# Halves of the tokens taking turns ahead of two wide attentions, in a one-core chain of eight sublayers

## Chip, cores and metric

The kernel runs on one core of a Trainium2 chip, in one launch. The metric is the device time of the launch in microseconds, as the median over runs.

## The reference, cut to what matters

1024 tokens (4 batches of 256) of width 128 pass through four gated pairs of cross attention and feed-forward. Every sublayer has the form `x = x + tanh(g) * f(...)`; the attentions and the first feed-forward work on a normalised x.

```python
x = x + tanh(g_xattn[1]) * L1_xattn(layernorm(x), ctx, mask, ...)   # 16 heads of 64: relu(scores)^2, normalised
x = x + tanh(g_ffn[1])   * L1_ffn(layernorm(x), ...)
x = x + tanh(g_xattn[2]) * L2_xattn(layernorm(x), ctx, ctx)         # 16 heads of 8, no weights
x = x + tanh(g_ffn[2])   * L2_ffn(layernorm(x), kernel, bias, a, b) # x @ (int4(kernel) + a @ b) + bias
x = x + tanh(g_xattn[3]) * L3_xattn(layernorm(x), ctx, ...)         # 16 heads of 64: clipped softmax
...
def L3_xattn(latents, context):
    lat, cx = layernorm(latents, ln_l_w, ln_l_b), layernorm(context, ln_c_w, ln_c_b)
    q, k, v = lat @ Wq, split(cx @ Wkv)
    attn = softmax(clip(q @ k.T * 64 ** -0.5, -11, 11))
    return (attn @ v) @ Wo + bo
```

L3_xattn normalises what it is given, so x is normalised twice there; the kernel does it in one norm with a changed epsilon.

## The kernel before

Each engine has its own program, in order, and semaphores tie them. The residual `res` lies tokens-first in eight tiles of 128 tokens; tiles 0 to 3 are the first half, 4 to 7 the second. Channels-first copies (`xf`, `xh`, `xl`) are 128x1024, a half is 512 columns. A product that must be precise takes three matmuls of split operands, high and low part (`mm3`, L185 to L189); `bank(k)` is one of eight PSUM banks of 512 columns.

A norm goes through five engines' queues. VectorE takes the statistics (`norm_sums`, L235), GpSimd the power (`norm_pool`, L271), VectorE a Newton step and the tiles (`norm_tiles`, L245), TensorE four transposes per half (`norm_pe`, L283), ScalarE a copy of the bank (`norm_act`, L302), and VectorE the low part (`norm_dve_split`, L315). `stream` (L278) is products of the identity with itself, whose result nobody reads. In these functions both halves go through a step before the next step begins.

A wide attention (call c = 0 for L1, c = 1 for L3) has 16 heads in eight pairs of heads by four batches: 32 groups g, two to a turn x, four turns to a weight block i. `project(x)` makes queries and keys of head pair x // 2 for half x % 2, in banks 6 and 7. ScalarE copies them as high parts (`high`, L1029), VectorE subtracts the low parts (`low`, L1142). `scores(g)` (L884) needs the queries and keys of batch g % 4, so groups 0 and 1 need the first half alone. VectorE bounds the scores (`bound`, L1151), ScalarE makes the weights (`weights`, L1050), TensorE the value products (L907), GpSimd adds the weights for the denominators (L1091). Ahead of the loop TensorE does

```python
            for h in range(2):
                pe.wait_ge(s_xs, 2 * splits(m) + h + 1)
                project(h)
            at("va", 2)
            scores(0)
            at("va", 4)
            scores(1)
            project(2)
```

VectorE does `low(0)`, `low(1)`, `bound(0)`, `bound(1)`, and ScalarE `high(0)`, `high(1)`, `weights(0)`, `weights(1)`. The attention adds its output into `xn`, which VectorE sets to zero (c = 0, L2101) or to the bias bo (c = 1, L2153) ahead of the loop.

Between the narrow attention L2 and the wide L3, TensorE transposes the normalised context (`context_pe`, L808), ScalarE applies weight and bias (L819, L820) and VectorE subtracts the low part (L824). The quantised feed-forward L2_ffn is eight products of 128 columns, each two records in the trace (L336); VectorE adds the bias (L2142), then the gated residual (L1246), then takes the statistics. These are norms 5 and 6, and the projections of the context's values (`wide_first_values_pe`, L863) stand behind both.

## Time and profile before

| | |
|---|---|
| median of 3 runs | 853.56 us (850.42 to 855.19) |
| the profiled execution | 858.75 us, its span 856.9 us |
| busy: TensorE, VectorE, ScalarE, GpSimd | 780.0, 626.2, 451.7, 197.0 us |
| first stretch (ahead of wide attention c = 0) | about 168 to 190 us |
| second stretch (ahead of wide attention c = 1) | about 519 to 551 us |
| GpSimd's additions L1091 | 64, mean 1358 ns |

The span is from the first to the last instruction of the profiled execution, and its own time includes what lies around that. Matmuls are pipelined and their ends modelled, so the busy time of TensorE (PE) is no peak rate. PEld is its weight load, DVE is VectorE, ACT ScalarE, POOL GpSimd. A bracket at a row's end names the idle time before the instruction and what ended it.

### The profile page before, as it was taken

How to read it: one execution, taken by the hardware profiler on the slowest of the kernel's cores; microseconds unless marked ns; L12 is line 12 of the kernel's file. 1: busy time of each engine (PE TensorE's matmuls, PEld its weight loads, DVE VectorE, ACT ScalarE, POOL GpSimd, SP SyncE). 2: the span in 40 equal slices, each digit the busy share in tenths (PEclk: the TensorE clock that was granted, in tenths of full speed). 3: DMA queues.
4: the chain of work that ended last, by engine and by line, in shares of the span. 5: the costliest groups of instructions: out<-in, count | busy, mean ns of one | idle time of the engine just before them, and what ended most of it. 6: DMA issues, size and time to landing. Idle time of an engine off the chain costs nothing. (4 is left out here: it accounts for less than half of the span.)

```text
span 856.9 us, 14220 instructions
## 1 busy us (share of the span) xinstructions
PE 780.0 (91%) x5206; PEld 556.2 (65%) x5206; DVE 626.2 (73%) x1168; ACT 451.7 (53%) x681; POOL 197.0 (23%) x163
## 2 busy tenths in 40 slices
PE   5998889989999899999989887899998879999996
PEld 4654556666677587777766545666775757777774
DVE  6678576667766587888776877776657868778876
ACT  3466352246655316999825665565554145555553
POOL 3000020023545321222220001146445201111112
PEclk9999789989999897999999999999999989999998
DMA  9100000130220200000270000002201000000000
GB/s 347 71 2 1 2 0 1 48 149 2 52 51 2 50 1 1 0 1 0 99 313 1 2 1 2 2 1 52 50 20 32 2 1 0 1 1 0 0 1 24
DMA packets 3660, 29.64 MB, mean 35 GB/s; under 512 B 560, under 2 KB 912, under 8 KB 2064
## 3 DMA queue, kind: packets, MB, share of 16 engines
q1 hardware_dynamic: 3600, 28.83, 10.0%
q8 instruction: 40, 0.66, 0.3%
q14 instruction: 20, 0.16, 0.1%
HBM read 28.20 MB, written 0.62 MB: 34 GB/s over the span
## 5 line engine op out<-in xcount | busy, mean ns | idle before, releaser
L187 PE MATMUL banks<-normed_t_high,work_split 128*128 128x512 f32 x250 | 110.1, 440 | 12.3 <-DVE work L1942 3.9
L1091 POOL TENSOR_TENSOR work<-work 128x512 f32<-128x512 f32 x64 | 86.2, 1358 | 134.0 <-ACT work L1053 134.0
L189 PE MATMUL banks<-normed_t_high,work_split 128*128 128x512 f32 x250 | 101.1, 404 | 0.0
L188 PE MATMUL banks<-normed_t_low,work_split 128*128 128x512 f32 x250 | 100.9, 404 | 0.0
L712 DVE TENSOR_REDUCE work<-banks 128x2 f32<-128x512 f32 x128 | 84.7, 688 | 18.3 <-PE banks L454 15.4
L1829 ACT ACTIVATE work<-banks 128x512 f32<-128x512 f32 x68 | 40.6, 598 | 70.2 <-PE banks L189 70.2
L276 POOL TENSOR_TENSOR ln_rstd<-ln_var_eps,minus_half_and_newton 128x4 f32<-128x4 f32 x16 | 17.2, 1076 | 248.3 <-DVE ln_var_eps L242 239.6
L1942 DVE TENSOR_TENSOR work<-work,banks 128x512 f32<-128x512 f32 x68 | 46.6, 687 | 36.0 <-ACT work L1829 35.6
L187 PEld LDWEIGHTS banks<-normed_t_high,work_split 128*128 128x128 f32 x250 | 48.0, 192 | 34.2 <-issue 17.6
L187 PE MATMUL banks<-work_split 128*128 128x512 f32 x148 | 64.2, 434 | 6.3 <-DVE work_split L1905 4.9
L907 PE MATMUL banks<-work 128*64 128x256 f32 x512 | 64.1, 388 | 2.2 <-ACT work L1053 1.7
L1688 DVE TENSOR_TENSOR work_split<-work,work_split 128x512 fp32r<-128x512 f32 x64 | 53.2, 832 | 16.0 <-ACT work_split L1614 15.3
L189 PE MATMUL banks<-work_split 128*128 128x512 f32 x148 | 58.5, 395 | 0.0
L188 PE MATMUL banks<-work_split 128*128 128x512 f32 x148 | 58.5, 395 | 0.0
L454 PE MATMUL banks<-work_split 32*128 32x256 f32 x256 | 54.1, 330 | 4.6 <-DVE work L712 3.0
L895 PEld LDWEIGHTS banks<-work_split 64*128 64x128 f32 x768 | 49.8, 194 | 12.7 <-issue 7.3
L1860 POOL TENSOR_TENSOR sublayer_out_t<-sublayer_out_t,work 128x512 f32<-128x512 f32 x18 | 23.6, 1312 | 148.6 <-DVE work L1916 146.7
L895 PE MATMUL banks<-work_split 64*128 64x256 f32 x768 | 56.5, 295 | 0.0
L188 PEld LDWEIGHTS banks<-normed_t_low,work_split 128*128 128x128 f32 x250 | 48.3, 193 | 12.1 <-issue 3.4
L189 PEld LDWEIGHTS banks<-normed_t_high,work_split 128*128 128x128 f32 x250 | 48.2, 193 | 11.7
L1053 ACT ACTIVATE work<-work,small_operands 128x1024 f32<-128x1024 f32 x32 | 36.8, 1150 | 34.7 <-DVE work L1157 34.1
L1145 DVE TENSOR_TENSOR work_split<-banks,work_split 128x512 fp32r<-128x512 f32 x32 | 21.8, 683 | 45.3 <-ACT work_split L1033 45.3
(288 smaller groups left out, 1752.6 us busy)
## 6 DMA issues: line engine op xcount, KB each, us to landing
raw_b<-in_wf SPq DMA_DIRECT2D x1, 6528.0 KB, 19.1
raw_a<-in_wf SPq DMA_DIRECT2D x1, 4096.0 KB, 13.1
raw_b<-reciprocal_rows SPq DMA_DIRECT2D x6, 512.0 KB, 6.0
raw_a<-reciprocal_rows SPq DMA_DIRECT2D x6, 512.0 KB, 6.4
raw_a<-in_wf SPq DMA_DIRECT2D x1, 2048.0 KB, 15.5
raw_b<-in_wb SPq DMA_DIRECT2D x1, 2048.0 KB, 19.7
raw_a<-in_wb SPq DMA_DIRECT2D x1, 2048.0 KB, 7.8
small_operands<-in_small SPq DMA_DIRECT2D x1, 1530.0 KB, 11.5
```

Source lines behind the costliest of these rows:

```text
L187: nc.tensor.matmul(o, w[0], m[0], start=start, stop=False)
L188: nc.tensor.matmul(o, w[0], m[1], start=False, stop=False)
L189: return nc.tensor.matmul(o, w[1], m[0], start=False, stop=stop)
L454: last = nc.tensor.matmul(ps[:, 7 - n % 2, e * S:(e + 1) * S], a_y[a_rows(j), t * P:(t + 1) * P], half(a_ky, x % 4)[a_rows(j), pair * S:(p ...
L712: nc.vector.tensor_reduce(a_nm[:, t:t + 2, j], bank(7 - n % 2).rearrange("p (e k) -> p e k", e=2), AX.X, ALU.max, negate=True).then_inc(A[ ...
L895: last = nc.tensor.matmul(ps[:, 2 * (g % 2) + h, kb * S:(kb + 1) * S], w_k[kt][rows, keys], w_q[qt][rows, b * S:(b + 1) * S], start=n == 0 ...
L907: last = nc.tensor.matmul(ps[DH * h:DH * (h + 1), 4, (b % 2) * S:(b % 2 + 1) * S], w_v[:, 2 * b + kb, (2 * p + h) * DH:(2 * p + h + 1) * D ...
L1053: nc.scalar.activation(p, p, func, bias=bias, scale=0.125).then_inc(W["p"].sem, 1)
L1091: nc.gpsimd.tensor_tensor(w_ps[g % 2].rearrange("p (h q) -> p h q", h=2), v[:, :, 0, :], v[:, :, 1, :], ALU.add).then_inc(W["ps"].sem, 1)
L1688: nc.vector.tensor_tensor(g_a[n % 4][1], g_af[n % 4], g_a[n % 4][0].bitcast(F32), ALU.subtract)\
L1829: nc.scalar.activation(k_sg[n % 2], bank(n % 2), ACT.Silu).then_inc(K["sg"].sem, 1)
L1942: nc.vector.tensor_tensor(k_af[n % 2], k_sg[n % 2], bank(2 + n % 2), ALU.mult).then_inc(K["a"].sem, 1)
```

## The change

In both stretches a half goes through all its steps before the other. Ahead of either wide attention TensorE transposes and projects the first half, then transposes the second, makes the scores of groups 0 and 1, and then projects the second half; the third projection follows the first value products inside the loop. VectorE's `low(1)` stands behind the first two bounds, and the clearing of `xn` behind the second weight block's split in the loop's first turn. ScalarE copies the first value tiles before the norm's halves. Between L2 and L3 the context's low part goes to GpSimd under its own semaphores; the bias of the quantised layer becomes a matmul of the identity with the broadcast bias, opening each bank's accumulation, and VectorE reads the sum straight into the residual (`back_half`). The order of norms 5 and 6 interleaves by half.

```diff
-        def context_low(dve, m, h):
-            dve.wait_ge(s_xf, 2 * m + h + 1)
-            nc.vector.tensor_tensor(half(cl, h), half(out_t, h), half(ch, h).bitcast(F32), ALU.subtract).then_inc(s_xs, 1)
+        def context_low(pool, h):
+            pool.wait_ge(s_cf, h + 1)
+            nc.gpsimd.tensor_tensor(half(cl, h), half(out_t, h), half(ch, h).bitcast(F32), ALU.subtract).then_inc(s_cl, 1)
...
                 for k in range(4):
                     x = 4 * i + k
                     pair(x)
+                    if x == 0:
+                        project(2)
                     next_scores(x)
...
-            for h in range(2):
-                pe.wait_ge(s_xs, 2 * splits(m) + h + 1)
-                project(h)
+
+            pe.wait_ge(s_ve, 2 * n + 1)
+            stream(6, 6)
+            norm_half_pe(pe, n, 0)
+            pe.wait_ge(s_xs, 2 * splits(m) + 1)
+            project(0)
+            stream(4, 5)
+            norm_half_pe(pe, n, 1)
             at("va", 2)
             scores(0)
             at("va", 4)
             scores(1)
-            project(2)
+            pe.wait_ge(s_xs, 2 * splits(m) + 2)
+            project(1)
...
-            for n in range(4):
-                value_tiles(n, n)
+            norm(0)
+            if c == 0:
+                norm(1)
             high(0)
+            if c == 1:
+                norm(1)
             high(1)
             weights(0)
             weights(1)
...
                     if x == 0:
                         wide_weights(dve, c, 1, raw, r0)
+                        clear()
...
             low(0)
-            low(1)
+            second()
             bound(0)
             bound(1)
+            low(1)
...
+        def quant_half_pe(pe, h):
+
+            pe.wait_ge(s_qw, 1)
+            pe.wait_ge(s_xf, 2 * 5 + h + 1)
+            nc.tensor.matmul(bank(6 + h).rearrange("p (t d) -> p t d", t=4), ident,
+                             col("quant_bias").unsqueeze(1).to_broadcast((P, 4, D)), start=True, stop=False)
+            for t in range(4):
+                last = nc.tensor.matmul(ps[:, 6 + h, t * P:(t + 1) * P], xf[:, (4 * h + t) * P:(4 * h + t + 1) * P],
+                                        q_w[:, :], start=False, stop=t == 3)
+            last.then_inc(s_rt, 1)
...
-            norm_pool(pool, 5)
-            norm_pool(pool, 6)
+            norm_half_pool(pool, 5, 0)
+            context_low(pool, 0)
+            norm_half_pool(pool, 5, 1)
+            norm_half_pool(pool, 6, 0)
+            context_low(pool, 1)
+            norm_half_pool(pool, 6, 1)
...
-            context_act(act, 5)
-            norm_act(act, 6, k=4, done=2 * splits(5))
-            norm_act(act, 7, w=col("ln_l_w"), b=col("ln_l_b"), k=4)
-            wide_act(act, 1, ACT.Exp, 0.0)
+            norm_half_act(act, 5, 0)
+            context_act(act)
+            wide_first_tiles_act(act, 1, 0)
+            norm_half_act(act, 5, 1)
+            wide_first_tiles_act(act, 1, 1)
...
-            order.step(nc.vector.memset(xn[:, :, :], 0.0))
...
+            dve.wait_ge(A["att"].sem, A["att"].at(1, NG, 0))
+            tokens_in(dve, order, 4, a_att, (1,))
+            norm_sums(dve, order, 5, 1, res)
+            back_half(dve, order, 3, 5, 0)
+            norm_sums(dve, order, 6, 0, res)
+            norm_tiles(dve, order, 5, 1, res, xn)
+            norm_tiles(dve, order, 6, 0, res, xn)
+            back_half(dve, order, 3, 5, 1)
+            norm_sums(dve, order, 6, 1, res)
+            norm_half_split(dve, order, 6, 0, xh, xl, False)
+            norm_tiles(dve, order, 6, 1, res, xn)
...
-            norm_pe(pe, 5, 6, k=4)
-            pe.wait_ge(s_qw, 1)
-            tokens_pe(pe, xf, q_w[:, :], ((s_xf, 2 * 6 + 1), (s_xf, 2 * 6 + 2)))
-            pe.wait_ge(s_xs, 2 * splits(5) + 2)
-            wide_first_values_pe(pe, 1)
-            norm_pe(pe, 6, 7, k=4)
-            wide_pe(pe, 1, 7, raw_a, RB3)
+            quant_half_pe(pe, 0)
+            wide_first_values_pe(pe, 1, 0)
+            stream(6, 7)
+            norm_half_pe(pe, 5, 1)
+            quant_half_pe(pe, 1)
+            wide_first_values_pe(pe, 1, 1)
+            wide_pe(pe, 1, 6, 6, raw_a, RB3)
```

The order on TensorE before, at the start of the first wide attention, from the last matmul of the second projection on (L189 of mm3 ends a projection, L895 are scores, L907 value products, L926 denominators):

```order
L189 MATMUL banks<-context_t_high,work_split 128x512
L895 MATMUL banks<-work_split 128x256 x24
L187 MATMUL banks<-normed_t_high,work_split 128x512
L188 MATMUL banks<-normed_t_low,work_split 128x512
L189 MATMUL banks<-normed_t_high,work_split 128x512
L187 MATMUL banks<-context_t_high,work_split 128x512
L188 MATMUL banks<-context_t_low,work_split 128x512
L189 MATMUL banks<-context_t_high,work_split 128x512
L907 MATMUL banks<-work 64x256 x8
L895 MATMUL banks<-work_split 128x256 x24
```

The same place in the change, from the first projection's last matmul on (L284 is `stream`, L300 the transposes, L910 scores, L922 value products):

```order
L189 MATMUL banks<-context_t_high,work_split 128x512
L284 MATMUL banks<-small_operands 128x128 x4
L300 MATMUL banks<-small_operands,normed_tokens 128x128 x4
L910 MATMUL banks<-work_split 128x256 x24
L187 MATMUL banks<-normed_t_high,work_split 128x512
L188 MATMUL banks<-normed_t_low,work_split 128x512
L189 MATMUL banks<-normed_t_high,work_split 128x512
L187 MATMUL banks<-context_t_high,work_split 128x512
L188 MATMUL banks<-context_t_low,work_split 128x512
L189 MATMUL banks<-context_t_high,work_split 128x512
L922 MATMUL banks<-work 64x256 x8
L187 MATMUL banks<-normed_t_high,work_split 128x512
```

Each projection moved one place back: the second from ahead of the scores to behind them, the third (it begins in the last row) from ahead of the first value products to behind them.

VectorE in the loop's first turn of the first wide attention, before (L1145 and L1148 are low parts, L1157 bounds, L1130 and L1135 the weights' split):

```order
L1157 SCALAR_TENSOR_TENSOR work<-banks,score_floor,raw_b 128x1024 x2
L1130 CAST work_split<-raw_b 128x768
L1135 TENSOR_TENSOR work_split<-raw_b,work_split 128x768
L1145 TENSOR_TENSOR work_split<-banks,work_split 128x512
L1148 TENSOR_TENSOR work_split<-banks,work_split 128x512
```

And in the change:

```order
L1182 SCALAR_TENSOR_TENSOR work<-banks,score_floor,raw_b 128x1024 x2
L1155 CAST work_split<-raw_b 128x768
L1160 TENSOR_TENSOR work_split<-raw_b,work_split 128x768
L2155 MEMSET normed_tokens 128x1024
L1170 TENSOR_TENSOR work_split<-banks,work_split 128x512
L1173 TENSOR_TENSOR work_split<-banks,work_split 128x512
```

The memset came from ahead of the first low parts; in the second wide attention a copy of the bias bo takes the same place.

## Rows read from the trace of the kernel before

**Rows 1.** Page, part 1: busy time, share of the span, instructions.
```profile
PE 780.0 (91%) x5206; PEld 556.2 (65%) x5206; DVE 626.2 (73%) x1168; ACT 451.7 (53%) x681; POOL 197.0 (23%) x163
```

**Rows 2.** Waits of TensorE from 196 to 320 us: total, times, longest.
```profile
PE banks L934 <- DVE normed_t L1172: 3.2, 1, 3.2
PE banks L187 <- ACT work L1047: 0.8, 3, 0.3
```

**Rows 3.** Timeline of TensorE, first stretch: start us, us, engine, line, operation, operands, [idle before <-releaser].
```profile
177.84 1.10 PE L299 MATMUL banks<-small_operands,normed_tokens 128*128 128x128 f32 x4 [0.52 <-DVE normed_tokens L256]
...
179.21 0.50 PE L187 MATMUL banks<-normed_t_high,work_split 128*128 128x512 f32 x1 [0.27 <-DVE normed_t_low L322]
...
180.91 0.63 PE L189 MATMUL banks<-context_t_high,work_split 128*128 128x512 f32 x1
...
183.56 0.77 PE L187 MATMUL banks<-normed_t_high,work_split 128*128 128x512 f32 x1 [2.02 <-DVE work_split L1148]
...
185.83 0.63 PE L189 MATMUL banks<-context_t_high,work_split 128*128 128x512 f32 x1
...
186.38 1.86 PE L895 MATMUL banks<-work_split 64*128 64x256 f32 x24
...
190.24 2.28 PE L907 MATMUL banks<-work 128*64 128x256 f32 x16 [0.40 <-ACT work L1053]
```

**Rows 4.** Slices of 1 us: busy shares, PEclk (the granted clock), DMA.
```profile
179.00:180.00 1.00, 0.79 (x3) 0.67 (x4) 0.55 (x2) 1.00 (x3) 0.00 (x0) 0.97 0.09 33
...
186.00:187.00 1.00, 1.00 (x8) 0.62 (x8) 0.53 (x1) 0.51 (x1) 0.00 (x0) 0.62 0.00 0
```

**Rows 5.** Timelines of VectorE and ScalarE, first stretch, by start.
```profile
179.47 2.06 ACT L1047 ACTIVATE work<-banks 128x512 f32<-128x512 f32 x4
...
180.46 0.91 DVE L2101 MEMSET normed_tokens<- 128x1024 f32 x1 [0.16 <-issue]
...
187.73 2.47 DVE L1157 SCALAR_TENSOR_TENSOR work<-banks,score_floor,raw_b 128x1024 f32<-128x1024 f32 x2
...
189.04 2.34 ACT L1053 ACTIVATE work<-work,small_operands 128x1024 f32<-128x1024 f32 x2 [1.95 <-DVE work L1157]
```

**Rows 6.** Timeline of TensorE, second stretch.
```profile
523.23 4.18 PE L281 MATMUL banks<-small_operands 128*128 128x128 f32 x36
...
528.63 2.02 PE L336 MATMUL banks<-quant_weights,normed_t 128*128 128x128 f32 x16
...
533.45 0.39 PE L187 MATMUL banks<-work_split,context_t_high 128*128 128x256 f32 x1 [2.80 <-DVE context_t_low L824]
...
542.37 0.50 PE L187 MATMUL banks<-normed_t_high,work_split 128*128 128x512 f32 x1 [1.62 <-DVE normed_t_low L322]
...
543.63 0.40 PE L189 MATMUL banks<-context_t_high,work_split 128*128 128x512 f32 x1
...
551.03 2.21 PE L907 MATMUL banks<-work 128*64 128x256 f32 x16 [0.41 <-ACT work L1053]
```

**Rows 7.** Timeline of VectorE, second stretch.
```profile
522.24 0.26 DVE L734 RECIPROCAL work<-banks 128x16 f32<-128x16 f32 x1 [2.76 <-PE banks L504]
...
528.30 0.69 DVE L824 TENSOR_TENSOR context_t_low<-sublayer_out_t,context_t_high 128x512 fp32r<-128x512 f32 x1
...
529.79 0.69 DVE L2142 TENSOR_TENSOR normed_tokens<-banks,small_operands 128x512 f32<-128x512 f32 x1 [0.80 <-PE banks L336]
...
543.29 0.69 DVE L2153 COPY normed_tokens<-small_operands 128x1024 f32<-128x1024 f32 x1
```

**Rows 8.** Durations of VectorE's split and tile lines, ns min/median/max, first and last start.
```profile
L1135 DVE TENSOR_TENSOR work_split<-raw_b,work_split x4: 957/1474/1927, 167.4 to 244.4; 128x768 fp32r<-128x768 f32 x4
...
L256 DVE TENSOR_SCALAR normed_tokens<-residual,ln_mean_var,ln_rstd x64: 328/344/1065, 6.8 to 680.6; 128x128 f32<-128x128 f32 x64
```

**Rows 9.** Timeline of TensorE at 168 us; the page's group of GpSimd's addition.
```profile
167.93 1.88 PE L1425 MATMUL banks<-work_split,small_operands 128*128 128x512 f32 x4
...
L1091 POOL TENSOR_TENSOR work<-work 128x512 f32<-128x512 f32 x64 | 86.2, 1358 | 134.0 <-ACT work L1053 134.0
```

More of the change, by code:

```diff
@@ L296, in norm_pe @@
             for h in range(2):
-                for t in range(4 * h, 4 * h + 4):
-                    pe.wait_ge(s_xn, NT * n + t + 1)
-                    last = nc.tensor.transpose(ps[:, k + h, (t % 4) * P:(t % 4 + 1) * P], src[:, t, :], ident)
-                last.then_inc(s_xt, 1)
-        def norm_act(act, m, f32=True, high=None, w=None, b=None, k=6, done=None):
-            for h in range(2):
-                act.wait_ge(s_xt, 2 * m + h + 1)
-                act.wait_ge(s_xs, 2 * splits(m) if done is None else done)
-                if f32 and w is None:
-                    ins = nc.scalar.activation(half(xf, h), bank(k + h), ACT.Copy)
-                elif f32:
-                    ins = nc.scalar.activation(half(xf, h), bank(k + h), ACT.Identity, bias=b, scale=w)
-                if high is not None:
-                    ins = nc.scalar.activation(half(high, h), bank(k + h), ACT.Copy)
-                ins.then_inc(s_xf, 1)
+                norm_half_pe(pe, n, h, src, k)
@@ new lines, in norm_half_pe, with norm_act, norm_half_act @@
+        def norm_half_pe(pe, n, h, src=xn, k=4):
+            for t in range(4 * h, 4 * h + 4):
+                pe.wait_ge(s_xn, NT * n + t + 1)
+                last = nc.tensor.transpose(ps[:, k + h, (t % 4) * P:(t % 4 + 1) * P], src[:, t, :], ident)
+            last.then_inc(s_xt, 1)
+        def norm_act(act, m, f32=True, high=None, w=None, b=None, k=6):
+            for h in range(2):
+                norm_half_act(act, m, h, f32, high, w, b, k)
+        def norm_half_act(act, m, h, f32=True, high=None, w=None, b=None, k=4):
+            act.wait_ge(s_xt, 2 * m + h + 1)
+            act.wait_ge(s_xs, 2 * splits(m))
+            if f32 and w is None:
+                ins = nc.scalar.activation(half(xf, h), bank(k + h), ACT.Copy)
+            elif f32:
+                ins = nc.scalar.activation(half(xf, h), bank(k + h), ACT.Identity, bias=b, scale=w)
+            if high is not None:
+                ins = nc.scalar.activation(half(high, h), bank(k + h), ACT.Copy)
+            ins.then_inc(s_xf, 1)
@@ L325, in back_pe, with norm_half_split @@
+        def norm_half_split(dve, order, m, h, hi, lo, from_bank=True, k=4):
+            dve.wait_ge(s_xf, 2 * m + h + 1)
+            src = bank(k + h) if from_bank else half(xf, h)
+            if not from_bank:
+                order.step(nc.vector.tensor_copy(half(hi, h), src))
+            nc.vector.tensor_tensor(half(lo, h), src, half(hi, h).bitcast(F32), ALU.subtract).then_inc(s_xs, 1)
         def back_pe(pe, ready, k):
@@ L1135, in wide_weights_low, with wide_dve @@
             nc.vector.tensor_tensor(w_w[i % 2][1], qkv, w_w[i % 2][0].bitcast(F32), ALU.subtract).then_inc(W["w"].sem, 1)
-        def wide_dve(dve, order, c, raw, r0, between, spare):
+        def wide_dve(dve, order, c, raw, r0, second, clear, between, spare):
             def at(name, n):
@@ L2170, in _ @@
             f0_pe(pe, 1)
-            wide_first_values_pe(pe, 0)
-            norm_pe(pe, 2, 2, k=4)
-            wide_pe(pe, 0, 2, raw_b, RB1)
+            for h in range(2):
+                wide_first_values_pe(pe, 0, h)
+            wide_pe(pe, 0, 2, 2, raw_b, RB1)
             norm_pe(pe, 3, 3)
```

97 lines of the change are left out of this document (42 added, 55 removed).

## The prediction

> **What bounds the kernel now.** I read the page first: TensorE is busy 780.0 of 856.9 us [rows 1]. That mean hides two kinds of place, so the waits of TensorE came next. From 196 to 320 us, which is most of a wide attention, its only long wait is 3.2 us near the attention's end [rows 2]; inside the loop over head pairs it hardly waits. So whatever delays the first pair delays the end one for one, and a head start is kept if nothing is added to the loop. The two stretches that the change rewrites lie before those loops: about 170 to 190 us, and 519 to 551 us. I walked both in the timelines, engine by engine.
>
> First stretch. TensorE transposes the second half while VectorE makes the first half's low part, projects the first half at 179.21, waits 2.02 us, projects the second at 183.56, scores from 186.38 and reaches the first value products at 190.24 [rows 3]. ScalarE's weights start at 189.04, as soon as VectorE's bound of the first scores (187.73, two in 2.47) is through [rows 5]. The granted clock is 0.97 and then lower in the slices from 179 us on, 0.62 as it comes back in slice 186 [rows 4]: between them the engine runs at 1.2 GHz. So the second projection lasts from 183.56 to 186.46, where six such products at 2.4 GHz take from 542.37 to 544.03, 1.66 us [rows 3, 6]; the first, 179.21 to 181.54, took 2.33 us [rows 3]. Together 1.9 us of this stretch is clock.
>
> Second stretch. VectorE is the chain: context's low part at 528.30, the bias added at 529.79 after waiting 0.80 for the quantised product, then the two halves' statistics and tiles until 539.6 [rows 7]. TensorE fills in with 36 records of identity products in 4.18 us (18 products of 0.23), waits 2.80 before 533.45, projects at 542.37 and reaches the first values at 551.03 [rows 6].
>
> **The sum, first stretch (+4.0 us).** Nothing before 179.21 moves: the same low part releases the same projection. Behind it now stand four identity products (0.93) and the second half's four transposes (0.7 with their tail), so these end at 179.21 + 1.40 + 0.93 + 0.7 = 182.3 at 2.4 GHz. ScalarE copies the second half, then query and key, at about 0.5 apiece [rows 5]; VectorE's three subtractions at some 0.61 apiece (0.69 alone, [rows 7]) end at 184.8. Scores start there, 1.5 us earlier than now. But the second projection stands behind both scores (1.62) and ends at 188.1, and on ScalarE the copies of that projection stand in front of the first weights: these start at 188.6, though their scores were bounded by 187.0. First values: 189.8 against 190.24, a gain of only 0.45. Then the third projection comes between the first values and the next scores: before, it ran in TensorE's wait, now it adds its whole 1.40. VectorE's bound of the next scores stands behind the low parts of that projection, which wait for ScalarE's copies of it: +0.4. The clearing of the tokens (0.91) stood in a wait of VectorE [rows 5] and now stands in the loop's first turn, behind the next weights' split, with the next low parts and bounds queued behind it: +0.9. Sum at 2.4 GHz: -0.45 + 1.40 + 0.4 + 0.9 = +2.3. I take the low clock to come back: TensorE does less ahead of 179.9 us than now, as the second half's transposes (1.10 us, [rows 3]) have gone from there. That gives back 1.7 of the 1.9 us, which the -0.45 had counted as gained. **+4.0**; ends: +2.3 (full clock) and +4.6 (clock low as long as now, scores and copies in it too).
>
> **The sum, second stretch (-2.4 us).** The first half's tiles for the quantised layer go into VectorE's 2.76 us wait for the last transposes [rows 7]: free. Transposes and ScalarE's copy (behind the context tiles) end at 523.8. The bias now costs TensorE a product of its own per half: two 128x512 products in plain float32 show as four records in 1.88 us, so 0.94 each [rows 9]; I take 0.9, bounded below by 0, if it fits a wait, and above by twice that at half clock. With four products of 0.25 the first half is back at 525.7 (now 529.65). VectorE then needs 0.79 for the residual, 1.40 for the statistics and, with the second half's tiles at 1.75, is at 529.7. Two subtractions of 0.6 and two bias additions of 0.7 have left it, 2.6 us. GpSimd's low part has no row of its own: the nearest is its 128x512 addition, mean 1.358 [rows 9]; lower bound 0.69, VectorE's own price [rows 7], upper bound 1.36 + 0.96 if it meets a VectorE instruction. It ends at 526.4, and the second half's power behind it on GpSimd at 527.5, before VectorE asks for it at 527.9: covered by 0.4 us. Transpose, copy, bias and products of the second half end at 532.5; then the second values (1.4), six identity products (1.4, and these, not data, are late next) and the first half's transposes to 535.9, ScalarE 0.8, VectorE's cast and low part 1.15: the first projection at 537.9 against 542.37, 4.5 earlier. The tail of the first stretch follows: scores at 540.9, second projection 542.8 to 544.5, first values at 546.2 against 551.03, 4.85 earlier. Then the loop takes +1.40 and +0.4 as above, and the bias copy (0.69, [rows 7]) that moves into it +0.7. **-2.4**; upper end -1.2, if the second context subtraction on GpSimd holds the tiles.
>
> That end is from rows: one tile instruction takes 344 ns in the median and 1065 at most, the split 957 at least and 1927 at most, and the long ones lie beside instructions of GpSimd [rows 8]. I keep 1.25, one GpSimd instruction, as the bound and 0 as the value, since the second context subtraction can start as the tiles end. The Trainium skill, SBUF — State Buffer, SBUF: two separate sides, says that VectorE in a two-port mode or with two SBUF inputs and GpSimd exclude each other for a whole instruction. By that rule the sum would be 1.25 higher in the worst order of arrival; the doubled split agrees, what the order will be no row shows.
>
> **Together** +4.0 - 2.4 = +1.6 us. The profiled execution took 858.75 us, 5.2 above the median of 853.56; put on the median it gives **855.2**. The cases of the sum reach from -0.1 to +3.4. A measurement of this kernel can tell some 0.5%, 4.3 us, from no change, so this is no change, chance 0.50.
>
> **Rivals.**
> 1. The loop has room (0.15). The head starts stay and the moved projection and clearing are absorbed: -0.45 - 4.85 = -5.3, **848.2**. For it: TensorE's busy time has gaps of tenths. Against: no wait over 0.8 us until the attention's end [rows 2].
> 2. GpSimd blocks VectorE (0.13), which ends slower. Three places: the quantised layer's tiles (1.25) and, in each attention's first turn, the split and the clearing, which now stand in a row beside GpSimd's additions (1.26 each beyond the sum): +3.8 on +1.6, **859.0**. It decides if a GpSimd addition starts before each of these; for it, the split that doubles already [rows 8].
> 3. The clock falls in both stretches (0.15): before the first projection TensorE now waits 1.9 us in either. +0.6 in the first and +1.0 in the second: **856.8**, and with the hold of the tiles 858.
> 4. It does not do what it says (0.07): scores in the first stretch no earlier than 186.4, as the streams and the second half's transposes eat the lead; +1.5 more: 856.7.
>
> **Numbers.** Faster by over 0.5%: 0.13 of rival 1, 0.04 of the rest, 0.17. Slower: 0.10 of rival 2, 0.08 of rival 3, 0.04 of the rest, 0.22. Within: 0.61. The range 848.5 to 859.5 takes in rival 2 and the sum's ends, and stops just short of rival 1.
>
> **What would show it.** Right: in the first attention the first value products at 190 to 192 us, with ScalarE's two projection copies directly ahead of the first weights; a projection between the first values and the next scores; in the second attention the first projection near 538 us, the first values near 546 us and the second pair only some 3 us earlier than before. Wrong: if TensorE shows waits inside the loop's later turns, room was there; if the second pair in the first attention starts by 196.3 us, the inserted projection cost nothing; if VectorE's tiles or splits show 1 us and more beside GpSimd, rival 2 holds; if the granted clock is full from 179 to 187 us, take 1.7 off.

## The result, and the profile after

The changed kernel takes 860.78 us (median of 5 executions, 857.9 to 863.3) against 853.56 (850.42 to 855.67, now with 5 executions too): ratio 1.0085, interval 1.0056 to 1.0113. It is 7.2 us slower; the forecast was 855.2 and no change, and the range ended at 859.5.

| | before | after |
|---|---|---|
| median | 853.56 us | 860.78 us |
| the profiled execution, its span | 858.75, 856.9 us | 857.9, 856.0 us |
| busy TensorE, VectorE, ScalarE, GpSimd | 780.0, 626.2, 451.7, 197.0 us | 775.0, 626.9, 452.9, 199.2 us |
| mean granted clock of the profiled execution | 0.958 | 0.969 |

The two profiled executions are level, though the medians are 7.2 us apart: the one of before took 5.2 us more than the median of its kernel, at a low mean clock, and the one after was the fastest of its five. So the spans say nothing here, and I compare stretches between landmarks. A runs from the second instruction `ln_var_eps` of norm 2 on VectorE (175.12 us before, 168.99 after) to the first value products of the turns 0, 1, 2 and 4 of the wide attention c = 0; B from the last reciprocal of the narrow attention (522.24, 520.66) to the same of c = 1. The expectations call turn 2 the third pair and turn 4 the fifth pair, and A the stretch from the power, or from the second statistics, of norm 2.

| us from the landmark | A: turn 0 | 1 | 2 | 4 | B: turn 0 | 1 | 2 | 4 |
|---|---|---|---|---|---|---|---|---|
| before | 15.12 | 21.12 | 26.87 | 42.32 | 28.79 | 34.73 | 40.39 | 55.34 |
| after | 15.99 | 23.51 | 30.70 | 46.14 | 25.55 | 32.91 | 40.51 | 55.69 |

A is 3.8 us longer, B 0.3. In A the turns last the same in both kernels from turn 2 on (15.45 and 15.44 us from 2 to 4, and 86.5 and 86.4 from 4 to the last, turn 15): a delay is kept whole, and there is no room in the loop. In B they agree within 0.3 us up to turn 12 (116.8 and 117.1 us from the landmark); one late turn, described under "The change once more", then differs by 2.3 us.

TensorE in the first stretch after, timeline (start us, us, engine, line, operation, operands, [idle before <-releaser]; the view ends at 200 us, so its last row holds only the first products of turn 2):

```profile
178.74 2.93 PE L910 MATMUL banks<-work_split 64*128 64x256 f32 x24 [2.70 <-DVE work_split L1173]
181.61 0.50 PE L187 MATMUL banks<-normed_t_high,work_split 128*128 128x512 f32 x1
...
184.98 2.12 PE L922 MATMUL banks<-work 128*64 128x256 f32 x16 [1.72 <-ACT work L1075]
187.03 0.50 PE L187 MATMUL banks<-normed_t_high,work_split 128*128 128x512 f32 x1
...
188.64 1.70 PE L910 MATMUL banks<-work_split 64*128 64x256 f32 x24
...
192.50 2.27 PE L922 MATMUL banks<-work 128*64 128x256 f32 x16
...
199.69 0.65 PE L922 MATMUL banks<-work 128*64 128x256 f32 x4 [0.65 <-ACT work L1075]
```

Against [rows 3]: the scores start 9.75 us after the landmark instead of 11.26, the 1.5 us that the forecast had. But that is clock and not order: the profile of before had 6.8 us of low clock, nearly all of it ahead of its scores (179 to 187 us), this one has none there. A later run ("Second stretch changed, with the copy ahead of the loop") has the old order in A and saw no low clock:

```profile
181.78 1.70 PE L910 MATMUL banks<-work_split 64*128 64x256 f32 x24
...
185.64 2.27 PE L922 MATMUL banks<-work 128*64 128x256 f32 x16 [0.56 <-ACT work L1089]
```

Its landmark is at 172.51 us, so at full clock the old order reaches the scores after 9.27 us, 0.5 earlier than the new. The reason shows in the first row after: TensorE waits 2.70 us for VectorE, whose low parts of the first projection stand behind the low part of the second half, and that began at 176.71 us, when ScalarE had copied the half. The scores then last 2.93 us instead of 1.86, since the granted clock is 0.50 in the slices of 179 and 180 us. The first values then wait 1.72 us for ScalarE, and the third projection (187.03) pushes the next scores back by its 1.6 us. ScalarE says why the values wait:

```profile
182.60 0.60 ACT L1056 ACTIVATE work_split<-banks 128x512 fp32r<-128x512 f32 x1 [4.95 <-PE banks L189]
183.30 0.60 ACT L1058 ACTIVATE work_split<-banks 128x512 fp32r<-128x512 f32 x1
183.79 2.18 ACT L1075 ACTIVATE work<-work,small_operands 128x1024 f32<-128x1024 f32 x2
```

It stood idle for 4.95 us, copied the second projection, and only then made weights whose bounds VectorE had started at 180.44. VectorE in the first turn, where [rows 5] answers:

```profile
192.95 1.92 DVE L1160 TENSOR_TENSOR work_split<-raw_b,work_split 128x768 fp32r<-128x768 f32 x1
195.03 0.91 DVE L2155 MEMSET normed_tokens<- 128x1024 f32 x1 [0.16 <-issue]
195.97 0.69 DVE L1170 TENSOR_TENSOR work_split<-banks,work_split 128x512 fp32r<-128x512 f32 x1
...
197.18 2.47 DVE L1182 SCALAR_TENSOR_TENSOR work<-banks,score_floor,raw_b 128x1024 f32<-128x1024 f32 x2
```

The second stretch. TensorE, to set beside [rows 6]:

```profile
522.08 1.10 PE L1766 MATMUL banks<-small_operands 128*128 128x512 f32 x2
...
529.27 0.59 PE L300 MATMUL banks<-small_operands,normed_tokens 128*128 128x128 f32 x2 [0.95 <-DVE normed_tokens L256]
...
537.87 0.50 PE L187 MATMUL banks<-normed_t_high,work_split 128*128 128x512 f32 x1 [2.06 <-DVE normed_t_low L329]
...
546.21 2.03 PE L922 MATMUL banks<-work 128*64 128x256 f32 x16 [1.63 <-ACT work L1075]
...
559.04 0.47 PE L187 MATMUL banks<-normed_t_high,work_split 128*128 128x512 f32 x1 [1.16 <-DVE work_split L1173]
```

VectorE and GpSimd there, to set beside [rows 7]:

```profile
523.39 1.24 DVE L242 TENSOR_SCALAR ln_var_eps<-ln_mean_var 128x4 f32<-128x4 f32 x1
...
527.33 2.14 DVE L256 TENSOR_SCALAR normed_tokens<-residual,ln_mean_var,ln_rstd 128x128 f32<-128x128 f32 x4
...
529.96 1.12 DVE L256 TENSOR_SCALAR normed_tokens<-residual,ln_mean_var,ln_rstd 128x128 f32<-128x128 f32 x4
...
553.96 1.91 DVE L1160 TENSOR_TENSOR work_split<-raw_a,work_split 128x768 fp32r<-128x768 f32 x1
555.80 1.78 DVE L2191 COPY normed_tokens<-small_operands 128x1024 f32<-128x1024 f32 x1
```

```profile
523.34 1.27 POOL L831 TENSOR_TENSOR context_t_low<-sublayer_out_t,context_t_high 128x512 fp32r<-128x512 f32 x1 [5.08 <-ACT context_t_high L827]
...
527.87 1.26 POOL L831 TENSOR_TENSOR context_t_low<-sublayer_out_t,context_t_high 128x512 fp32r<-128x512 f32 x1
...
553.50 3.52 POOL L1116 TENSOR_TENSOR work<-work 128x512 f32<-128x512 f32 x2 [4.76 <-ACT work L1075]
```

Three instructions of VectorE are long where GpSimd works: one of four columns takes 1.24 us, and ends as GpSimd's subtraction ends, four tiles take 2.14 where the next four take 1.12, and the copy of the bias takes 1.78 where it took 0.69 [rows 7]. The first projection stands at 537.87, the very time of the forecast, but this is chance: the landmark itself stands 1.6 us earlier in this trace, and from the landmark its gain is 2.9 us, not 4.5.

### The profile page after: what moved, and what is told of

It reads as the page before. It is cut to its first block and busy times, and to the rows that moved or that the text cites. A ratio compares the mean times of both kernels' runs of the same rounds, so it can differ in the third digit from the quotient of the medians.

```text
span 856.0 us, 14196 instructions
## 1 busy us (share of the span) xinstructions
PE 775.0 (91%) x5194; PEld 550.0 (64%) x5194; DVE 626.9 (73%) x1164; ACT 452.9 (53%) x681; POOL 199.2 (23%) x165
## 5 line engine op out<-in xcount | busy, mean ns | idle before, releaser
L189 PE MATMUL banks<-normed_t_high,work_split 128*128 128x512 f32 x250 | 100.9, 404 | 0.0
L922 PE MATMUL banks<-work 128*64 128x256 f32 x512 | 64.5, 388 | 6.6 <-ACT work L1075 6.1
L910 PEld LDWEIGHTS banks<-work_split 64*128 64x128 f32 x768 | 50.5, 196 | 15.2 <-issue 9.9
L910 PE MATMUL banks<-work_split 64*128 64x256 f32 x768 | 57.1, 297 | 2.9 <-DVE work_split L1173 2.9
L189 PE MATMUL banks<-work_split 128*128 128x512 f32 x148 | 58.2, 394 | 0.0
L189 PEld LDWEIGHTS banks<-normed_t_high,work_split 128*128 128x128 f32 x250 | 48.4, 194 | 11.8
L922 PEld LDWEIGHTS banks<-work 128*64 128x64 f32 x512 | 32.8, 137 | 35.9 <-ACT work L1075 20.4
```

The source lines that it names most:

```text
L189: return nc.tensor.matmul(o, w[1], m[0], start=False, stop=stop)
L910: last = nc.tensor.matmul(ps[:, 2 * (g % 2) + h, kb * S:(kb + 1) * S], w_k[kt][rows, keys], w_q[qt][rows, b * S:(b + 1) * S], start=n == 0 ...
L922: last = nc.tensor.matmul(ps[DH * h:DH * (h + 1), 4, (b % 2) * S:(b % 2 + 1) * S], w_v[:, 2 * b + kb, (2 * p + h) * DH:(2 * p + h + 1) * D ...
```

## The experiments

**My theory**: the loss is the first stretch's new order; in the second the interleaving gains, and GpSimd beside VectorE and the copy inside the loop give it back. **Rivals**: the loss sits in the second stretch or behind it; it is the projection inside the loop alone; or it is clock, not order. The medians of the kernel before, taken beside the groups of runs, were 853.73, 855.58, 855.0 and 854.13 us, so the ratios are the better figures.

**Only the second stretch changed.** The wide attention c = 0 goes in the order of before.

```diff
-                    if x == 0:
+                    if x == 0 and c == 1:
                         project(2)
...
+            if c == 0:
...
+                norm_half_pe(pe, n, 0)
+                norm_half_pe(pe, n, 1)
+                for h in range(2):
+                    pe.wait_ge(s_xs, 2 * splits(m) + h + 1)
+                    project(h)
...
```

> The first wide attention starts in its old order (both halves transposed, both projected, scores, third projection, clearing ahead of the first low parts); the second stretch stays as changed. Theory A, the loss sits in the first stretch (the projection between first values and next scores, the clearing in the loop's first turn): from the power of norm 2 to the third pair of values it takes 26.8 us as before instead of 30.6, and the whole kernel falls by 3.5 to 4 against the change, to some 1 us above before. Rival B, the loss sits in the second stretch or spread by the clock: the time stays within 1.5 us of the change.

Measured: 855.43 us, ratio 1.0009 (0.9984 to 1.0033); A 41.91, B 55.66 us to turn 4. The loss goes with the first stretch, and the second alone brings nothing. (B grew by 0.3 us, as in the change.)

**Only the first stretch changed**, the opposite edit, on the kernel before.

```diff
+            if c == 0:
+                pe.wait_ge(s_ve, 2 * 2 + 1)
+                stream(6, 6)
+                transposes(0)
+                pe.wait_ge(s_xs, 2 * splits(m) + 1)
+                project(0)
+                stream(4, 5)
+                transposes(1)
...
```

> The kernel before with the new start of the first wide attention alone (second half's transposes behind the first projection, scores ahead of the second projection, third projection and clearing inside the loop). My theory (the first stretch carries the whole loss): ratio 1.005 to 1.007, 4 to 6 us slower than before, and 46 us from the second statistics of the norm to the pair with index 4 against 42.3 in the kernel before (the second stretch's 55.3 us unchanged). Rival (the loss needs both stretches, or comes from how they meet with the clock): 0 to 2 us slower, ratio up to 1.002, although the first stretch is longer.

Measured: 859.66 us, 4.7 more than before, ratio 1.0064 (1.0039 to 1.0089); A 48.01, B 55.35 us. That is the theory's case; A is even 5.7 us longer than before. Its TensorE meets the low clock twice (3.4 us each; before had 6.8 us in one piece), granted clock in slices of 1 us (us, PE busy, PEclk, DMA):

```profile
177.00:178.00 1.00, 1.00 (x6) 0.50 0.00 0
179.00:180.00 1.00, 0.53 (x5) 1.00 0.00 0
...
183.00:184.00 1.00, 1.00 (x13) 0.50 0.00 0
```

**Clearing and copy ahead of the loop**, both attentions.

```diff
                         wide_weights(dve, c, 1, raw, r0)
-                        clear()
...
             low(1)
+            clear()
```

> The change with the clearing of the tokens moved from behind the second weight block's split to behind the third low part, just ahead of the loop, where VectorE idles 4.1 us (first attention) and 3.6 us (second). Theory A, the clearing delays the loop: the memset took 0.94 and the bias copy 1.78 us (it met GpSimd's additions), so the third pair comes 0.9 earlier in the first attention and 1.8 earlier in the second, the whole falls by 2.7. Rival B, the split beside GpSimd is what delays the second turn and the clearing hides behind it: under 1 us together.

Measured: 860.5 us, ratio 1.0087 (1.0059 to 1.0114); A 45.07, B 53.86 us, so 1.07 and 1.83 us less to turn 4 than in the change. The copy takes its old time again, with GpSimd idle beside it:

```profile
547.77 0.68 DVE L2191 COPY normed_tokens<-small_operands 128x1024 f32<-128x1024 f32 x1
```

The stretches are shorter as the theory had it, while the median did not show the 2.9 us. It had only 6 executions, at a mean granted clock of 0.962 where the kernel before had 0.965, so the expected 2.7 us can be neither seen nor ruled out in it.

**The first weights ahead of the second projection's copies** on ScalarE, on top of that.

```diff
-            high(1)
             weights(0)
             weights(1)
+            high(1)
```

> As the run with the clearing ahead, and ScalarE makes the first two groups' weights before it copies the second projection. Theory A, the weights stand behind the copies of the second projection: first values 1.2 to 1.5 us earlier in either attention, but the third projection then waits for the low parts of the second, so about 0.5 us of that is kept in each, 1 us in all below the run with the clearing ahead. Rival B, TensorE has room elsewhere: the whole 1.2 is kept in each, 2.5 in all. Rival C: the copies come so late that the loop loses 0.5.

Measured: 856.08 us, ratio 1.0027 (1.0005 to 1.0049), the best kernel that has the new order in both attentions, and 4.4 us below the run with the clearing alone, where 1 us was expected (2.6 us when both are put on one clock, as below). A 45.65 with the low clock twice, B 53.80 us. In B the first values start 1.1 us earlier than with the clearing alone (24.46 against 25.54), but turn 1 stands at 32.85 against 32.89: the second projection's copies, now behind, take the head start back. So the traces show no gain of this size in B, and what the rest of it is stays open.

**The third projection ahead of the first values**, on top of the clearing ahead.

```diff
                     pair(x)
-                    if x == 0:
-                        project(2)
...
             project(1)
+            project(2)
```

> The run with the clearing ahead, and the third projection stands before the first value products again, behind the second projection, in both attentions. It must wait there for the second projection's low parts, which come about when the first weights do. Theory A, the inserted projection is the largest term (1.4 us of products plus 0.4 to 1.3 for VectorE's bounds that wait behind it): from norm 2's power to the fifth pair 43.5 to 44 us instead of 45.07, in the second stretch 52.5 to 53 instead of 53.86, and 2 to 3 us in all below the run with the clearing ahead. Rival B, it only changes places with the first values, as the low parts come late: within 0.5 us of the run with the clearing ahead.

Measured: 858.77 us, ratio 1.0046 (1.0013 to 1.0078), one far outlier among its executions left out; B 55.26 us. The median is 1.7 us below the run with the clearing alone (0.8 on one clock), less than theory A's 2 to 3 us. From the landmark of B the first values are 2.6 us later than with the clearing alone (28.10 against 25.54), and turn 2 is 1.5 later (40.29 against 38.77); but this run met a low clock just there, from 551 to 555 us, and the other did not. The third projection, to the first values, takes 2.29 us there against 1.56 in its own A, and the turn behind it 6.52 against 5.67; without these 1.6 us turn 2 would stand at 38.7, level with the clearing alone (an estimate). So in B the projection only changes places with the first values, rival B: ahead of them it waits for low parts that the new order makes late. TensorE in A, with 1.50 us of waiting that the kernel before did not have there:

```profile
191.59 0.47 PE L187 MATMUL banks<-normed_t_high,work_split 128*128 128x512 f32 x1 [1.50 <-DVE work_split L1172]
...
193.15 1.95 PE L922 MATMUL banks<-work 128*64 128x256 f32 x16
```

**Context's low parts back on VectorE**, the rest as changed.

```diff
-            nc.gpsimd.tensor_tensor(half(cl, h), half(out_t, h), half(ch, h).bitcast(F32), ALU.subtract).then_inc(s_cl, 1)
+            nc.vector.tensor_tensor(half(cl, h), half(out_t, h), half(ch, h).bitcast(F32), ALU.subtract).then_inc(s_cl, 1)
...
```

> The change with the context's low parts back on VectorE (the first ahead of the first half's residual, the second behind the tiles of norm 6), everything else as changed. Theory A, GpSimd's low parts hold VectorE for about 1 us each (the epsilon instruction took 1.24 instead of 0.17, four tiles 2.14 instead of 1.12): without them the tiles take 1.12, but the two subtractions cost 0.6 each on VectorE, so first values move by -0.5 to +0.5. Rival B, moving them to GpSimd was worth its full 1.2 us: first values 1.2 us later than in the change.

Measured: 860.23 us, ratio 1.0072 (1.0036 to 1.0108); A 48.01 with the low clock twice, B 54.18 us, 1.5 less than in the change. The expectation was too small here: what left VectorE's queue (two of 0.68) came back to it as blocking. Without GpSimd the instructions have their old lengths:

```profile
523.41 0.17 DVE L242 TENSOR_SCALAR ln_var_eps<-ln_mean_var 128x4 f32<-128x4 f32 x1
525.36 1.12 DVE L256 TENSOR_SCALAR normed_tokens<-residual,ln_mean_var,ln_rstd 128x128 f32<-128x128 f32 x4
...
529.18 0.68 DVE L831 TENSOR_TENSOR context_t_low<-sublayer_out_t,context_t_high 128x512 fp32r<-128x512 f32 x1
...
560.03 1.78 DVE L2191 COPY normed_tokens<-small_operands 128x1024 f32<-128x1024 f32 x1
```

The copy, left inside the loop, keeps its 1.78: another cause, GpSimd's additions.

**The bias added on VectorE again**, out of PSUM.

```diff
-            nc.tensor.matmul(bank(6 + h).rearrange("p (t d) -> p t d", t=4), ident,
-                             col("quant_bias").unsqueeze(1).to_broadcast((P, 4, D)), start=True, stop=False)
...
+                order.step(nc.vector.tensor_tensor(r.rearrange("p (t d) -> p t d", t=4), bank(6 + h).rearrange("p (t d) -> p t d", t=4),
+                                                   col("quant_bias").unsqueeze(1).to_broadcast((P, 4, D)), ALU.add))
```

> The change with the quantised layer's bias added by VectorE again (written to the free channels-first tile, then the gated residual), and no bias product on TensorE. TensorE is shorter by 0.9 per half, VectorE longer by 0.7. Theory A: in the second stretch the two cancel, within 0.5 us of 55.69 to the fifth pair. Rival B, the bias product hid in waits: 1.4 us longer than the change.

Measured: 861.23 us, ratio 1.0074 (1.0043 to 1.0106); B 58.16 us, 2.5 more than in the change, part of it a low clock that lasts 6.8 us in this stretch (534 to 542 us). Ahead of that clock the first half's residual sum starts 0.8 us later than in the change (4.72 against 3.89 us from the landmark). So bias in PSUM is the better of the two by about that much in the trace, though the medians do not tell them apart (861.23 against 860.78 and 861.35); it is not where the time went.

**More identity products ahead of the first scores**, so that TensorE idles less there.

```diff
             norm_half_pe(pe, n, 0)
+            if c == 0:
+                stream(7, 5)
...
             norm_half_pe(pe, n, 1)
+            if c == 0:
+                stream(8, 4)
```

> The change with seven identity products more ahead of the first projection and eight more ahead of the first scores, in the first attention only, where TensorE waited 1.9 and 2.7 us. Theory A, part of the first stretch's loss is the low clock behind these waits: the stretch from norm 2's power to the fifth pair takes 44.5 to 45 instead of 46.14 and of 48.0 as in the run with the low parts on VectorE, the mean granted clock rises by 0.003, the whole falls by 1 to 2 us. Rival B, the clock falls behind transposes and identity products whatever their number: no change, or up to 0.5 us slower by late products.

Measured: 858.99 us, ratio 1.0021 (0.9991 to 1.005), not apart from before, and 1.8 us below the change's first median. In A the clock stayed full up to the first values, which gives the new order's price at full clock, but then fell:

```profile
180.84 1.70 PE L910 MATMUL banks<-work_split 64*128 64x256 f32 x24 [0.91 <-DVE work_split L1177]
...
185.86 2.81 PE L922 MATMUL banks<-work 128*64 128x256 f32 x16 [1.72 <-ACT work L1079]
188.60 0.80 PE L187 MATMUL banks<-normed_t_high,work_split 128*128 128x512 f32 x1
```

First values after 14.78 us (15.99 in the change), turn 4 after 46.52 (46.14): the low clock moved 6.5 us on and cost about as much. (B took 57.28 us, with a low clock from 542 to 546 us.) The profile alone would speak for rival B. The 12 executions do not: their mean granted clock is 0.969, the highest of all the kernels here, against 0.965 and 0.967 in the change and 0.964 in the kernel before beside it, and the time fell by the 1 to 2 us that theory A expected. About 1.2 to 1.9 us of the gain over the change is this clock by the slope given below; the profiled execution just did not show it.

**Second stretch changed, with the copy ahead of the loop**; the first as before.

The edit is shown against the run with only the second stretch changed.

```diff
-                        if c == 1:
-                            clear()
...
+            if c:
+                clear()
```

> The first stretch as before, the second as changed but with the clearing ahead of the loop. The second stretch takes 53.86 us from the last normalisation of the narrow attention to the fifth pair, 1.5 less than before (55.34), the first 42.3 less clock differences; whole time 1.8 below the run with only the second stretch changed, so some 1 to 1.5 us below before. Rival (clock): no difference from the run with only the second stretch changed.

Measured: 854.54 us, ratio 0.9992 (0.9961 to 1.0024); B 53.86 us, 1.5 less than before. The median is 0.9 us below the run with only the second stretch changed, where 1.8 was expected, which is within the noise. Its A saw no low clock at all and is the old order's price at full clock: first values after 13.13, turn 4 after 40.33 us.

**The same with the context's low parts on VectorE**, the best that the runs point to.

```diff
+                    if x == 0 and c == 1:
                         project(2)
...
+            context_low(dve, 0)
             back_half(dve, order, 3, 5, 0)
...
+            if c == 1:
+                low(1)
+            if c:
+                clear()
```

> The first wide attention starts in the order of before (both projections, then scores; third projection ahead of the first values; clearing ahead of the first low parts). The second stretch is as changed, but with the context's low parts back on VectorE and the copy of the bias ahead of the loop. My theory (the first stretch's new order is the loss; in the second, GpSimd's low parts and the copy inside the loop give back what the interleaving gained): from the last reciprocal of the narrow attention to the pair with index 4 it takes 52.4 us (53.9 with the copy alone moved, 55.3 in the kernel before), and the whole 2 to 3 us less than before, ratio 0.997. Rival (the low parts on GpSimd are hidden, and what they gained in the changed kernel came from another clock): 53.9 us and ratio 0.999 to 1.0. A ratio of 1.003 or more would say that the loss is not in the first stretch.

Measured: 854.85 us, ratio 0.9999 (0.9967 to 1.0032). A miss in the time: nothing won that can be measured. In B, 53.98 us, the instructions did what they should (1.12 for the tiles, 0.69 for the copy), but the first projection fell into a low clock:

```profile
535.00:536.00 1.00, 1.00 (x3) 0.63 0.03 8
536.00:537.00 1.00, 1.00 (x4) 0.50 0.00 0
538.00:539.00 1.00, 1.00 (x8) 0.67 0.00 0
```

Its first values come after 25.62 us where the run with the low parts on VectorE, at full clock there, had 24.05; take that 1.57 off and B is 52.4, the expected figure. Its mean granted clock over 12 executions is 0.960, the lowest of all kernels once the outlier named above is left out. So the work got shorter in the trace, and by the adjustment below the clock took it back; that the kernel itself brings the lower clock is not shown.

**The change once more.**

> The changed kernel once more, in more executions, beside the kernel before on one chip. If the parts add up (first stretch alone +4.7 us, second stretch alone +0.8 us), it is 5.5 us slower, ratio 1.0064, and the 7.2 us of its first five executions were partly chance. If it comes out at 7 us or more again, ratio 1.0080 or above, about 1.7 us come from how the two stretches meet, most likely by the clock.

Measured: 861.35 us (860.63 to 863.34), ratio 1.0091 (1.0062 to 1.0119): the 7 us are no chance of the first five executions. This time its profile met the low clock twice in A, as the run with the first stretch alone had:

```profile
175.54 0.63 PE L189 MATMUL banks<-normed_t_high,work_split 128*128 128x512 f32 x1
...
182.16 2.93 PE L910 MATMUL banks<-work_split 64*128 64x256 f32 x24 [2.70 <-DVE work_split L1173]
185.01 0.75 PE L187 MATMUL banks<-normed_t_high,work_split 128*128 128x512 f32 x1
...
188.65 2.12 PE L922 MATMUL banks<-work 128*64 128x256 f32 x16 [1.72 <-ACT work L1075]
```

A takes 47.98 us, 5.66 more than before with as long a low clock in it (6.8 us each), B 55.64, 0.30 more. Together 6.0 of the 7.2 us.

One more place differs, outside both stretches, where nothing was changed. Late in the attention c = 1, from turn 13 to 14, the two profiles of the change take 11.98 and 11.45 us, that of before 9.63, that of the second stretch alone 8.64. VectorE waits there for the reciprocals of the denominators, which a DMA writes to DRAM and a second one spreads over the partitions. The first of them, 16 KB, in the window from 630 to 650 us, in the change and in the kernel before (KB, and us from issue to landing), and then VectorE's wait in both:

```profile
reciprocal_rows<-normed_t SPq DMA_DIRECT2D x1, 16.0 KB, 3.6
...
reciprocal_rows<-normed_t SPq DMA_DIRECT2D x1, 16.0 KB, 1.7
...
647.68 1.76 DVE L1199 RECIPROCAL normed_t<-banks 128x256 f32<-128x256 f32 x1 [4.67 <-DMA raw_a<-reciprocal_rows]
...
647.71 1.76 DVE L1174 RECIPROCAL normed_t<-banks 128x256 f32<-128x256 f32 x1 [3.43 <-DMA raw_a<-reciprocal_rows]
```

From its issue to the issue of the transfer that waits for it, 3.62 and 3.26 us pass in the two profiles of the change and 3.55 with the clearing alone ahead, but 1.71 to 1.78 in the ten others, five of which have the new order in both attentions too. What delays it no run shows, nor whether the unprofiled executions have it.

**All executions together.** One line through 212 executions (all but the far outlier), with a level for each kernel and one slope for all, gives 4.7 us less for each 0.01 of mean granted clock. Put on one clock (0.966), the kernel before stands at 853.5 to 854.2 us in its groups, and the others at: best version 851.7, second stretch with the copy ahead 853.3, second stretch alone 854.8, weights first 856.2, third ahead 858.0, clearing ahead 858.8, first stretch alone 858.9, low parts on VectorE 859.4, more identity products 859.4, the change 860.5 and 861.9, bias on VectorE 861.5; each with a standard error of about 0.5, with 5 or 6 executions 0.7. This orders the kernels as their stretches do. It is an adjustment, not a measurement of a time that anyone gets.

**The first stretch at like clock**, from the profiles above, us from the landmark of A:

| order in A, low clock met | scores | turn 0 | turn 4 |
|---|---|---|---|
| old, none | 9.27 | 13.13 | 40.33 |
| old, 6.8 us in one piece (before) | 11.26 | 15.12 | 42.32 |
| new, none up to turn 0 (more identity products) | 9.76 | 14.78 | 44.9 (estimate) |
| new, 3.4 us (the change) | 9.75 | 15.99 | 46.14 |
| new, 3.4 us twice (the change once more) | 11.36 | 17.85 | 47.98 |

The estimate adds the 30.15 us that the change takes from turn 0 to turn 4 at full clock. At like clock the new order never has its scores earlier, and it is 4.6 us longer to turn 4 at full clock (an estimate) and 5.66 us longer with 6.8 us of low clock.

## Why the prediction was wrong

- **The path.** Right: in both kernels the turns behind the second are equal, and what the first two lose is kept. Rival 1 (room in the loop) has fallen.
- **First stretch, +4.0 us: nearly right, its upper end too low.** The 1.5 us of head start for the scores were the missing low clock, as the table above shows, and not the order; the forecast, too, took 1.7 us back as clock. First values at full clock after 14.78 us, where the forecast's 189.8 is 14.7; behind them it had +2.7 (1.40, 0.4, 0.9) and the two turns show +2.96. The profile after shows +3.8 with one low stretch of clock, its twin +5.66 with two, the first stretch alone +4.7 in the median. The upper end, 4.6, assumed that a low clock as long as before's 6.8 us costs no more than before. It costs more in the new order: 6.8 us of low clock move the first values from 13.13 to 15.12 us in the old order and from 14.78 to 17.85 in the new, 2.0 against 3.1. Likely this is because transposes, scores and the second projection now stand in one chain; no run isolates it.
- **Second stretch, -2.4 us: this is the step that failed.** It measured +0.3 in the profiles and +0.8 in the median of the second stretch alone. Two terms were wrong. The head start: 4.85 us was forecast, 3.24 came. With the low parts on VectorE it is 4.74 (28.79 less 24.05), but that nearness is partly luck: the run still has the two subtractions (1.4 us) in VectorE's queue, which the forecast had taken out. "0 as the value" for GpSimd beside the tiles was the error, 1.0 us there and 1.07 on the four-column instruction, which stood in no bound. And the loop: +2.5 was forecast, +3.36 came; the copy of the bias was priced at 0.69, from a place where GpSimd was idle, and cost 1.78. With the copy ahead of the loop B falls by 1.83 us, and with the low parts on VectorE by 1.51.
- **Rival 2** (GpSimd blocks VectorE, chance 0.13) was nearest in its mechanism, and half wrong in its places: tiles and copy were held, for about 1.1 us each, but in the first attention the split took 1.92 us both before and after, and the memset 0.91 in either place, the second time beside an addition of GpSimd. It gave 859.0; its price lay in the second stretch alone.
- **Rival 3** (the clock falls in both stretches) was right for the first, where its +0.6 was too little (the upper end of 4.6 against 5.66); in the second, neither profile of the change met a low clock. Its 856.8 held too little for it.
- **The uneven part.** The two stretches add to 5.5 us in medians (4.7 and 0.8), the change has 7.2. The clock-adjusted levels leave a gap of the same kind, with an uncertainty of about 0.8. Chance is not ruled out: the intervals of the two parts (up to 1.0089 and 1.0033) leave room for the whole 1.0085. In the profiles the late transfer of the reciprocals, described above, is 1.5 to 1.9 us longer in the change than with either stretch alone, which is of this size. That the stretches meet through the clock is possible too; no run decides, and it stays open.
- **The sum as such**: +1.6 forecast; with 4.7 and 0.8 in its terms' places it would have been +5.5, and 859.1 us, just inside the range. So the second stretch's terms were 3.2 us of the miss of 5.6, the first's 0.7, and the uneven part the remaining 1.7. The chance for slower, 0.22, was too small for a change whose every gain stood in one term beside a GpSimd instruction.

The Trainium skill, SBUF — State Buffer, SBUF: two separate sides, has GpSimd and VectorE exclude each other for a whole instruction; the trace agrees, with 1.24 against 0.17 us where one ends with the other. It names VectorE instructions in a two-port mode or with two SBUF inputs, and the trace agrees here too as far as it goes: the tiles, the copy and the split were held, the residual's sum out of PSUM was not (0.74 us beside GpSimd's power, 0.75 without).

## What to carry to other kernels

When turns are interleaved to start one part earlier, follow the queue of each engine up to the second turn: here, at full clock, the scores came 0.5 us later and not earlier, since VectorE met the second half's norm in front of them, and the first values 1.6 us later, since ScalarE met the second projection's copies in front of them. Price an instruction that moves by its new neighbours, not by its old duration; a subtraction of 0.69 us moved to GpSimd cost VectorE 1.07 us. And where the clock's low stretches come and go between executions, compare landmarks, put two low-clock cases side by side, and compare full clock with full clock, before believing a span or a head start.

## What the runs showed of the hardware that was not expected

- An instruction of VectorE over four columns, one input, waits out a whole GpSimd subtraction (1.24 us for 0.17). A memset of 1024 columns does not: 0.91 us beside one of GpSimd's additions and 0.91 with GpSimd idle.
- With fifteen identity products more in two waits, the one profile only moved the low stretch 6.5 us on, while the mean granted clock of 12 executions was the highest of all kernels, 0.969. The version with the shortest adjusted time had the lowest, 0.960.
- The clock can fall without a long wait: in the profile of before it fell at 179.9 us, where TensorE's longest idle time since 168 us was 0.52 us [rows 3]. In the run "Second stretch changed, with the copy ahead of the loop", with the same order there, it stayed full.
- A DMA of 16 KB took 1.7 us to land in one profile and 3.6 in another, at the same place of the program.
- A low clock costs far less than its length: 0.01 of the mean clock is 17 us at half clock in a span of 856, and costs 4.7 us by the line through the executions. Read directly, 6.8 us of it cost 2.0 us in the old order of A and 3.1 in the new.
- The same kernel, unchanged, spreads over 850 to 863 us, and its mean granted clock goes with it.
